# Projections of an adaLN layer: the first scale and shift applied after the transpose, by ScalarE, instead of before it, by VectorE

## The chip, the cores and the metric

One NeuronCore of a Trainium2 chip runs the whole kernel. The metric is the device time of one execution in microseconds (us), the median of several runs.

## The reference

Two adaLN layers on x of 2 batches of 2048 tokens, 256 features. Only the head of layer 0 matters here:

```python
mod = (silu(L0_c) @ L0_wmod).reshape(2, 6, 1, 256)   # L0_c is 2 x 256, L0_wmod 256 x 1536
sa, ca, ga, sb, cb, gb = mod[:, 0], ..., mod[:, 5]
h = layernorm(x) * (1 + ca) + sa                     # one scale and one shift a batch and feature
Q, K, V = h @ W_q.T, h @ W_k.T, h @ W_v.T            # then rotary embedding on Q and K
```

Causal attention with 16 heads of 16 features, a top-1 mixture of experts, and layer 1 (a Toeplitz mix and a top-2 mixture of experts) follow. All inputs are float32. Matrix products are made of rounded parts: a value is split into a part rounded to fp32r and the rest (`HI`, `LO`), and three of the four products are summed.

## The kernel before, in words

The program is a row of stages, each a block in which the five engines (TensorE: PE, VectorE: DVE, ScalarE: ACT, GpSimd: POOL, SyncE: SP, which issues most DMAs) run their own lists of instructions in order and meet by semaphores. The stages are `projections`, `attention`, `output_projection`, `top1_experts`, `layer1`, `routed_experts`, `combine`. The change lies in `projections` (L236 to L593) alone.

This stage works through 8 chunks of 512 tokens (4 a batch), each held as 4 tiles of 128 tokens by 256 features. For chunk i:

- DVE `statistics(i)` takes mean and variance (L372, then small ones at L142 to L148); POOL `deviation(i)` (L345) makes 1/sqrt.
- DVE `norm(i)` calls `normalize`: four `tensor_scalar` (L183) subtract the mean and divide, then `tensor_tensor` over 128x1024 multiplies by the scale (L187) and another adds the shift (L188). Scale and shift lie in `mods[0]`, the same row on all 128 partitions.
- PE `turn(i)` (L525) transposes the 8 blocks of h into the PSUM tile `p_t` (features on partitions, tokens along the row).
- ACT `round_hT(i)` (L457) copies `p_t` to `hT` HI, rounding; DVE `rest_of_hT(i)` (L391) subtracts HI from `p_t` to give LO.
- PE `product(i, qk)` (L537) makes q (qk 0) or k (qk 1) in 24 matmuls of 512 columns, 12 for each of the two summands `s` of the rotation; and V (L557), 24 of 256 columns.
- DVE `rotate` (L398) multiplies the PSUM result by cos or sin; POOL `add` (L334) sums the two into `rem`; then `rem` is split in three bf16 parts by ACT (L472), DVE `split` (L405), ACT (L476) and POOL `split_off` (L340). SP stores parts (L301) and V (L296) to HBM.

The order on DVE in `chunk(i)` is: norm(i+1), split(i-1, 1), rotate(i, 0) twice, rest_of_hT(i+1), statistics(i+2), rotate(i, 1) for s 0, split(i, 0), rotate(i, 1) for s 1. ACT does round_hT(i+1), take_v(i) (L465), then the splits; in chunks 4 to 6 it then issues the loads for the first stage of attention (`load_first_stage`), which need the stored parts of batch 0. PE does product(i, 0), V(i), turn(i+1), product(i, 1). In the first chunk all of these wait in addition for the start-up work.

Start-up: SP loads c, the first third of wmod (L311), x, the weights, the other two thirds of wmod, and the tables. DVE spreads silu(c) over 128 columns (`cb`, four `tensor_scalar` of 128x128 at L429), so that PE's products with wmod (L581, float32, 512 of its columns for each n of `halves`, in four passes) come out alike on all partitions; they are written to `pm`, which is the PSUM tile of V, and ACT copies them to `mods[0]` (L500). There are six such halves: (b, 0) gives sa and ca, (b, 1) ga and sb, (b, 2) cb and gb. Four are made before turn(0), two after it. PE's V product of chunk 0 waits until all are copied. `add_one` (L376) adds one to ca, later to cb.

At the end of the stage the first 12 maxima of attention (`early_maxima`) are already made, on data that the ACT-issued loads bring.

Of the kernel before, what the change touches and what calls it, by code (L numbers as in the profile page):

```python
# [25 lines left out]
P = 128  # L26
KT = D // P
CH = 512
# [150 lines left out]
def normalize(nc, k, own, i, h, scale, shift, done):  # L179


    for u in range(TPC):
        own.add(nc.vector.tensor_scalar(h[:, u, :], k.x[:, at(i * TPC + u, 1, 1), :].rearrange("p o d -> p (o d)"),  # L183
                                        k.mean[:, at(i * TPC + u, 1, 1)], k.rstd[:, at(i * TPC + u, 1, 1)],
                                        ALU.subtract, ALU.mult))
    own.wait()
    own.step(nc.vector.tensor_tensor(h, h, scale, ALU.mult))  # L187
    nc.vector.tensor_tensor(h, h, shift, ALU.add).then_inc(done, 1)  # L188
# [43 lines left out]
def projections(nc, a, k):  # L232

    with ExitStack() as stack:
# [18 lines left out]
        cT, silu_c = (small[:, 2 * P + n * KT * B:2 * P + (n + 1) * KT * B].rearrange("p (k b) -> p k b", k=KT) for n in range(2))  # L253
        pm = p_v[:, :, :].rearrange("p u d -> p (u d)").rearrange("p (n c) -> p n c", n=2)
        early = [p_t[:, :, :], p_qk[:, 0, :, :]]
        halves = [(0, 0), (1, 0), (0, 1), (0, 2), (1, 1), (1, 2)]
        c_loaded, wm_loaded = m.sem("c_loaded"), [m.sem(f"wm_loaded{n}") for n in range(2)]
        constants_loaded, x_in = m.sem("constants_loaded"), [m.sem(f"x_in{i}") for i in range(NCH)]
        c_ready, cb_ready, mod_ones_set = m.sem("silu_c_ready"), m.sem("cb_ready"), m.sem("mod_ones_set")
# [23 lines left out]
        def last_chunk(i):  # L283
            return i == NCH - 1

        with nc.Block() as block:
# [78 lines left out]
            def _(dve):  # L365
# [9 lines left out]
                def add_one(which):  # L375
                    c.step(nc.vector.tensor_scalar(k.mods[0][:, :, which, :], k.mods[0][:, :, which, :], 1.0, None, ALU.add))  # L376

                def norm(i):
                    dve.wait_ge(rstd_ready, i + 1)
                    if not first(i):  # L380
                        dve.wait_ge(turned, i)
                    normalize(nc, k, c, i, h[:, :, :], k.mod(0, i // CPS, CA), k.mod(0, i // CPS, SA), h_ready)

                def rest_of_w(n):
                    cols = columns[n]
# [2 lines left out]

                def rest_of_hT(i, par):
                    dve.wait_ge(hT_high, i + 1)  # L390
                    nc.vector.tensor_tensor(hT[:, par, LO, :, :], p_t[:, :, :], hT[:, par, HI, :, :],  # L391
                                            ALU.subtract).then_inc(hT_ready, 1)

                def rotate(i, qk, halves_of):
# [13 lines left out]
                def chunk(i, par):  # L408
                    if not last_chunk(i):
                        norm(i + 1)  # L410
                    if first(i):
                        dve.wait_ge(trig_loaded, 16)
                    else:
                        split(i - 1, 1)
                    rotate(i, 0, range(2))
                    if not last_chunk(i):
                        rest_of_hT(i + 1, 1 - par)
                    if i + 2 < NCH:
                        statistics(i + 2)
                    rotate(i, 1, range(1))  # L420
                    split(i, 0)
                    rotate(i, 1, range(1, 2))

                nc.vector.memset(ones, 1.0).then_inc(mod_ones_set, 1)
                dve.wait_ge(mod_ones_set, 1)
                dve.wait_ge(c_ready, 1)
                for kt in range(KT):
                    for b in range(B):
                        nc.vector.tensor_scalar(cb[:, kt, b, :], ones, silu_c[:, kt, b:b + 1], None, ALU.mult).then_inc(cb_ready, 1)  # L429
                statistics(0)  # L430
                dve.wait_ge(mod_copied, B)
                add_one(CA)
                norm(0)
                rest_of_w(0)
                statistics(1)
# [5 lines left out]
                dve.wait_ge(constants_loaded, 16 * 2)  # L441
                c.add(nc.vector.tensor_copy(k.identb[:, :], k.ident[:, :]))
                c.add(nc.vector.tensor_copy(k.masks[:, :], masks))
                dve.wait_ge(mod_copied, len(halves))
                add_one(CB)
                all_chunks(chunk)
                for u in range(EARLY):
                    if u == 2:
# [4 lines left out]
            @block.scalar  # L453
            def _(act):
                def round_hT(i, par):
                    act.wait_ge(turned, i + 1)
                    nc.scalar.activation(hT[:, par, HI, :, :], p_t[:, :, :], ACT.Copy).then_inc(hT_high, 1)  # L457

                def take_v(i):
                    act.wait_ge(v_psum, i + 1)  # L460
# [41 lines left out]

                act.wait_ge(c_loaded, 16)
                nc.scalar.activation(silu_c, cT, ACT.Silu).then_inc(c_ready, 1)
                for n in range(B):
                    take_mods(n)
                act.wait_ge(w_loaded, 16)
                for cols in columns:
                    nc.scalar.activation(w[:, HI, :, cols], raw[:, :, cols], ACT.Copy).then_inc(w_high, 1)
                for n in range(B, 2 * B):  # L510
                    take_mods(n)
                round_hT(0, 0)
                for n in range(2 * B, len(halves)):
                    take_mods(n)
                all_chunks(chunk)

# [1 line left out]
            def _(pe):  # L518
# [23 lines left out]
                def chunk(i, par):  # L542
                    pe.wait_ge(hT_ready, i + 1)
                    if first(i):
                        pe.wait_ge(w_ready, 1)
                    product(i, par, 0)
                    if first(i):
                        pe.wait_ge(mod_copied, len(halves))
                        pe.wait_ge(w_ready, 3)
                    elif last_chunk(i):  # L550
                        product(i, par, 1)
                    if not first(i):
                        pe.wait_ge(va_ready, i)
                    for u in range(TPC):
                        for kt in range(KT):
                            for wp, hp in PRODUCTS:
                                last = nc.tensor.matmul(p_v[:, u, :], hT[:, par, hp, kt, u * P:(u + 1) * P],  # L557
                                                        w[:, wp, kt, 4 * D:5 * D],
                                                        start=(kt, wp, hp) == (0, HI, HI),
                                                        stop=(kt, wp, hp) == (KT - 1, LO, HI))  # L560
                    last.then_inc(v_psum, 1)
                    if not last_chunk(i):
                        turn(i + 1)
                        product(i, par, 1)
# [9 lines left out]

                def modulate(n):
                    b, half = halves[n]
                    pe.wait_ge(wm_loaded[half > 0], 16)
                    if n >= 2:
                        pe.wait_ge(mod_copied, n - 1)
                    for kt in range(KT):  # L580
                        last = nc.tensor.matmul(pm[:, n % 2, :], cb[:, kt, b, :], wm[:, kt, 2 * half * D:(2 * half + 2) * D],  # L581
                                                start=kt == 0, stop=kt == KT - 1)
                    last.then_inc(mod_product, 1)

                pe.wait_ge(cb_ready, KT * B)
                for n in range(2 * B):
                    modulate(n)
                pe.wait_ge(constants_loaded, 16 * 2)
                turn(0)
                for n in range(2 * B, len(halves)):  # L590
                    modulate(n)
                all_chunks(chunk)
                early_maxima()  # L593

# [1982 lines left out]
```

## Time and profile before

| What | us |
|---|---|
| median of 3 runs (2446.16 to 2450.19) | 2449.44 |
| profiled execution, its time | 2455.55 |
| its span | 2453.8 |
| busy in the span: PE | 2206.0 |
| DVE | 1715.6 |
| ACT | 1273.1 |
| POOL | 878.1 |

The span runs from the first to the last instruction of the profiled execution; 1.75 us lie outside it. The projections take about the first 188 us of the span. Busy time of PE is modelled for pipelined matmuls, so a busy PE may still have slack. A line of the timeline has the start and the length of an instruction (or of a merged run of alike ones, then with a count), its engine and line, the tiles written and read with their shapes, and in brackets how long the engine stood idle before it and what ended that. "ACTq", "SPq" and "POOLq" are the sequencers that issue DMAs. "PEld" is the load of weights into TensorE.

### The profile page before, as it was taken

The numbers are of one execution on the slowest core, as the hardware profiler recorded it, in microseconds if no ns is written. First come the engines' busy times: TensorE is split into PE (matmuls) and PEld (weight loads), VectorE is DVE, ScalarE is ACT, GpSimd is POOL, SyncE is SP. The second block draws the span as 40 slices with busy tenths as digits, with TensorE's granted clock in tenths as the row PEclk, the third lists the DMA queues.
The fourth block names the chain that finished last, engine by engine and source line by source line (L and its number), as shares of the span: only waits on it lengthen the run. The fifth ranks groups of instructions, "written<-read, shape, count | busy, mean of one in ns | idle before, by whom it ended". The sixth has DMA issues, their size and how long they took to land. (4 is left out here: it accounts for less than half of the span.)

```text
span 2453.8 us, 38931 instructions
## 1 busy us (share of the span) xinstructions
PE 2206.0 (90%) x12968; PEld 1400.8 (57%) x12968; DVE 1715.6 (70%) x2748; ACT 1273.1 (52%) x2452; POOL 878.1 (36%) x1057
## 2 busy tenths in 40 slices
PE   7878999999999999988999599963999999999991
PEld 5752333333333333326777456643888888888881
DVE  8968787878788787815788778774555555555566
ACT  3332767777677767773333244421555555555552
POOL 3543321313131220212555512454345444445350
PEclk9986999999999999998999798875999999999996
DMA  6499116345261711003000100013534443444326
GB/s 212 142 205 127 26 62 112 89 105 96 81 122 54 148 71 45 1 16 118 1 0 0 34 0 5 35 41 121 189 135 140 143 136 136 171 157 142 134 74 219
DMA packets 140246, 235.78 MB, mean 96 GB/s; under 512 B 14816, under 2 KB 105568, under 8 KB 138656
## 3 DMA queue, kind: packets, MB, share of 16 engines
q1 hardware_dynamic: 124416, 181.18, 21.4%
q0 software_dynamic: 14544, 48.05, 11.1%
q10 hardware_dynamic: 1104, 4.20, 1.2%
q8 instruction: 105, 1.72, 0.3%
q14 instruction: 77, 0.63, 0.1%
HBM read 150.58 MB, written 82.42 MB: 95 GB/s over the span
## 5 line engine op out<-in xcount | busy, mean ns | idle before, releaser
L228 DVE TENSOR_REDUCE tile_max<-p_m 128x2 f32<-128x1024 f32 (+1 forms) x628 | 642.5, 1065 | 137.1 <-PE p_m L220 69.2
L929 ACT ACTIVATE probs<-p_s 128x512 f32<-128x512 f32 (+3 forms) x1280 | 596.4, 534 | 242.4 <-PE p_s L834 237.0
L2210 PE MATMUL p_up<-f_xT,f_w 128*128 128x512 f32 (+1 forms) x2304 | 464.8, 351 | 7.1 <-DVE f_w L2344 3.6
L2210 PEld LDWEIGHTS p_up<-f_xT,f_w 128*128 128x128 f32 x2304 | 368.9, 189 | 59.6 <-issue 9.2
L776 POOL TENSOR_SCALAR_AFFINE_SELECT probs<-probs 128x128 f32<-128x128 f32 x512 | 145.9, 294 | 700.9 <-ACT probs L929 692.4
L834 PE MATMUL p_s<-qa,ka 99*128 99x512 bf16 (+3 forms) x1280 | 352.0, 351 | 13.2 <-ACT probs L929 6.9
L217 PE MATMUL p_m<-ka,qa 96*128 96x512 bf16 (+1 forms) x1256 | 353.0, 364 | 11.2 <-DVE tile_max L228 5.0
L2379 POOL TENSOR_TENSOR f_w<-f_raw,f_w 128x1024 fp32r<-128x1024 f32 x95 | 230.9, 2440 | 365.2 <-ACT f_w L2265 365.2
L848 PE MATMUL p_o<-probs,va 128*32 128x512 f32 (+3 forms) x2560 | 301.5, 541 | 1.3 <-issue 1.0
L2225 PE MATMUL p_y<-f_w,f_hidden 128*128 128x256 f32 x1872 | 252.5, 281 | 15.1 <-DVE f_y L2339 14.2
L2225 PEld LDWEIGHTS p_y<-f_w,f_hidden 128*128 128x128 f32 x1872 | 237.8, 188 | 30.0 <-issue 21.7
L217 PEld LDWEIGHTS p_m<-ka,qa 96*128 96x128 bf16 x1256 | 108.2, 99 | 238.0 <-DVE tile_max L228 133.9
L2326 DVE SCALAR_TENSOR_TENSOR f_gate<-p_up,f_b,f_gate 128x512 f32<-128x512 f32 (+1 forms) x192 | 124.7, 649 | 166.3 <-ACT f_gate L2278 162.9
L834 PEld LDWEIGHTS p_s<-qa,ka 99*128 99x128 bf16 x1280 | 110.5, 98 | 223.6 <-ACT probs L929 143.0
L2330 DVE TENSOR_TENSOR f_hidden<-f_gate,f_hidden 128x512 fp32r<-128x512 f32 (+1 forms) x192 | 141.7, 738 | 118.7 <-ACT f_hidden L2283 112.0
L2278 ACT ACTIVATE f_gate<-p_up,f_b 128x512 f32<-128x512 f32 (+1 forms) x192 | 116.3, 606 | 154.9 <-PE p_up L2210 148.3
L1283 PE MATMUL p_e<-w_expert,c_hT 128*128 128x512 f32 x768 | 195.1, 404 | 0.0
L2283 ACT ACTIVATE f_hidden<-f_gate 128x512 fp32r<-128x512 f32 (+1 forms) x192 | 105.9, 552 | 160.3 <-DVE f_gate L2326 157.0
L1283 PEld LDWEIGHTS p_e<-w_expert,c_hT 128*128 128x128 f32 x768 | 140.6, 190 | 29.6
L2265 ACT ACTIVATE f_w<-f_raw 128x1024 fp32r<-128x1024 f32 x144 | 150.5, 1045 | 2.7 <-DMA f_raw<-in_W 2.2
L1709 PE MATMUL p_uv<-l_xnT,w_uv 128*128 128x512 f32 x256 | 112.7, 597 | 0.0
L537 PE MATMUL p_qk<-hT,wqkv 128*128 128x512 f32 x384 | 96.0, 409 | 14.8 <-DVE rot L398 14.7
(278 smaller groups left out, 2625.4 us busy)
## 6 DMA issues: line engine op xcount, KB each, us to landing
x_slots<-mods SPq DMA_DIRECT2D x73, 516.0 KB, 4.3
f_raw<-in_W SPq DMA_DIRECT2D x24, 1024.0 KB, 11.2
f_raw<-in_W1a SPq DMA_DIRECT2D x23, 1024.0 KB, 6.4
f_raw<-in_W1b SPq DMA_DIRECT2D x23, 1024.0 KB, 8.7
qk_scr<-parts SPq DMA_DIRECT2D x48, 256.0 KB, 2.8
qa<-qk_scr POOLq DMA_DIRECT2D x42, 256.0 KB, 15.7
ka<-qk_scr POOLq DMA_DIRECT2D x42, 256.0 KB, 17.6
v_scr<-wqkv_raw SPq DMA_DIRECT2D x32, 256.0 KB, 3.8
```

The lines of the kernel that those rows point to most:

```text
L217: last = nc.tensor.matmul(out[:, hh, 0:width], qa[0:QROWS, hd, q0:q0 + P], ka[0:QROWS, hd, bank * CH:bank * CH + width], start=True, stop= ...
L228: return nc.vector.tensor_reduce(out=k.tile_max[:, 2 * hp:2 * hp + 2, i, bank], in_=products[:, :, 0:width], op=ALU.max, axis=AX.X)
L776: last = nc.gpsimd.affine_select(block_, block_, pattern=[[1, P]], compare_op=ALU.is_ge, fill=0.0, base=0, channel_multiplier=-1)
L834: nc.tensor.matmul(p_s[:, s_bank(x, buf), lo:CH], ka[buf][0:QROWS + SPLIT, h, j * P:(j + 1) * P], qa[buf][0:QROWS + SPLIT, h, c * CH + lo: ...
L848: last = nc.tensor.matmul(p_o[VW * h:VW * (h + 1), lo:CH], va[buf][:, j, VW * h:VW * (h + 1)], probs[:, (buf * UNITS + n) % NPROBS, h, lo: ...
L929: nc.scalar.activation(probs[:, (buf * UNITS + n) % NPROBS, h, lo:CH], p_s[:, s_bank(("exp", HG * n + h), buf), lo:CH], ACT.Exp, scale=DH ...
L1283: last = nc.tensor.matmul(out, hT[:, par, hp, kt, :], weights(wp, kt), start=(kt, wp, hp) == (0, HI, HI), stop=(kt, wp, hp) == (KT - 1, LO ...
L2210: last = nc.tensor.matmul(p_up[:, f % 2, ab, 0:size], w1[:, wh, ab * KT + kt, f * P:(f + 1) * P], xT[:, t % 2, xh, kt, 0:size], start=(kt, ...
L2225: last = nc.tensor.matmul(p_y[:, u, :], hidden[:, (FB * t + f) % NHID, hh, u * P:(u + 1) * P], w2[:, wh, f, :], start=(f, wh, hh) == (0, H ...
L2265: nc.scalar.activation(piece_part(q, HI), piece_raw(q, par), ACT.Copy).then_inc(w_high, 1)
L2330: nc.vector.tensor_tensor(hidden[:, (n - 1) % NHID, LO, 0:size], gate[:, f % 2, 0:size], hidden[:, (n - 1) % NHID, HI, 0:size], ALU.subtra ...
L2379: nc.gpsimd.tensor_tensor(piece_part(q, LO), piece_raw(q, t % 2), piece_part(q, HI), ALU.subtract).then_inc(w1_ready, 1)
```

## The change

In layer 0's first norm, h now holds only the normalized x. The scale and the shift are needed with features on partitions: `modT` (128 x 2 x 2 x 2). PE makes them directly as eight float32 products with two result columns each (wmod block as weights, silu(c) as the moving side), DVE copies them from PSUM and adds one to the scale. ACT, which took the transposed chunk with one rounding copy, now applies them with two `Identity` instructions of 128x512 (one for each half of the features, scale and shift as columns of one value a partition) into a new SBUF tile `whole_hT`, waits for both, and rounds from `whole_hT`; DVE takes the rest from `whole_hT`, no longer from the PSUM tile. The two halves (b, 0) are no longer made the old way. The other four are moved on PE behind product(0, 0), the four L429 instructions on DVE behind the casts of the constants, and `add_one(CB)` into chunk 0 behind rotate(0, 0).

```diff
-        halves = [(0, 0), (1, 0), (0, 1), (0, 2), (1, 1), (1, 2)]
+        halves = [(0, 1), (0, 2), (1, 1), (1, 2)]
+        modT = m.sb("modT", [P, 2, KT, B])
+        whole_hT = m.sb("whole_hT", [P, KT, CH])
+        p_modT = p_v[:, 0, 0:2 * KT * B].rearrange("p (w k b) -> p w k b", w=2, k=KT)
...
@@ DVE, norm(i) @@
-                    normalize(nc, k, c, i, h[:, :, :], k.mod(0, i // CPS, CA), k.mod(0, i // CPS, SA), h_ready)
+                    for u in range(TPC):
+                        t = i * TPC + u
+                        last = nc.vector.tensor_scalar(h[:, u, :], k.x[:, t, :], k.mean[:, t:t + 1], k.rstd[:, t:t + 1],
+                                                       ALU.subtract, ALU.mult)
+                    last.then_inc(h_ready, 1)
...
@@ DVE, rest_of_hT(i, par) @@
-                    nc.vector.tensor_tensor(hT[:, par, LO, :, :], p_t[:, :, :], hT[:, par, HI, :, :],
+                    nc.vector.tensor_tensor(hT[:, par, LO, :, :], whole_hT[:, :, :], hT[:, par, HI, :, :],
                                             ALU.subtract).then_inc(hT_ready, 1)
...
@@ DVE, chunk(i, par) @@
                     rotate(i, 0, range(2))
+                    if first(i):
+                        dve.wait_ge(mod_copied, len(halves))
+                        add_one(CB)
                     if not last_chunk(i):
                         rest_of_hT(i + 1, 1 - par)
...
@@ DVE, start-up @@
                 nc.vector.memset(ones, 1.0).then_inc(mod_ones_set, 1)
-                dve.wait_ge(mod_ones_set, 1)
-                dve.wait_ge(c_ready, 1)
-                for kt in range(KT):
-                    for b in range(B):
-                        nc.vector.tensor_scalar(cb[:, kt, b, :], ones, silu_c[:, kt, b:b + 1], None, ALU.mult).then_inc(cb_ready, 1)
+                dve.wait_ge(modT_product, 1)
+                nc.vector.tensor_scalar(modT[:, CA, :, :], p_modT[:, CA, :, :], 1.0, None, ALU.add).then_inc(modT_ready, 1)
+                nc.vector.tensor_copy(modT[:, SA, :, :], p_modT[:, SA, :, :]).then_inc(modT_ready, 1)
                 statistics(0)
-                dve.wait_ge(mod_copied, B)
-                add_one(CA)
                 norm(0)
...
                 c.add(nc.vector.tensor_copy(k.masks[:, :], masks))
-                dve.wait_ge(mod_copied, len(halves))
-                add_one(CB)
+                dve.wait_ge(mod_ones_set, 1)
+                for kt in range(KT):
+                    for b in range(B):
+                        nc.vector.tensor_scalar(cb[:, kt, b, :], ones, silu_c[:, kt, b:b + 1], None, ALU.mult).then_inc(cb_ready, 1)
                 all_chunks(chunk)
...
@@ ACT, round_hT(i, par) @@
+                    b = i // CPS
                     act.wait_ge(turned, i + 1)
-                    nc.scalar.activation(hT[:, par, HI, :, :], p_t[:, :, :], ACT.Copy).then_inc(hT_high, 1)
+                    if first(i):
+                        act.wait_ge(modT_ready, 2)
+                    else:
+                        act.wait_ge(hT_ready, i)
+                    for kt in range(KT):
+                        nc.scalar.activation(whole_hT[:, kt, :], p_t[:, kt, :], ACT.Identity, scale=modT[:, CA, kt, b:b + 1],
+                                             bias=modT[:, SA, kt, b:b + 1]).then_inc(modulated, 1)
+                    act.wait_ge(modulated, KT * (i + 1))
+                    nc.scalar.activation(hT[:, par, HI, :, :], whole_hT[:, :, :], ACT.Copy).then_inc(hT_high, 1)
...
@@ ACT, start-up @@
-                for n in range(B):
-                    take_mods(n)
...
-                for n in range(B, 2 * B):
-                    take_mods(n)
                 round_hT(0, 0)
-                for n in range(2 * B, len(halves)):
+                for n in range(len(halves)):
                     take_mods(n)
...
@@ PE, chunk(i, par) @@
                     product(i, par, 0)
                     if first(i):
+                        pe.wait_ge(cb_ready, KT * B)
+                        pe.wait_ge(modT_ready, 2)
+                        for n in range(len(halves)):
+                            modulate(n)
                         pe.wait_ge(mod_copied, len(halves))
                         pe.wait_ge(w_ready, 3)
...
@@ PE, start-up @@
-                pe.wait_ge(cb_ready, KT * B)
-                for n in range(2 * B):
-                    modulate(n)
+                pe.wait_ge(c_ready, 1)
+                pe.wait_ge(wm_loaded[0], 16)
+                for which in (SA, CA):
+                    for mb in range(KT):
+                        col = which * D + mb * P
+                        for kt in range(KT):
+                            last = nc.tensor.matmul(p_modT[:, which, mb, :], wm[:, kt, col:col + P], silu_c[:, kt, :],
+                                                    start=kt == 0, stop=kt == KT - 1)
+                last.then_inc(modT_product, 1)
                 pe.wait_ge(constants_loaded, 16 * 2)
                 turn(0)
-                for n in range(2 * B, len(halves)):
-                    modulate(n)
                 all_chunks(chunk)
```

## Rows read from the trace of the kernel before

**Rows 1.** One stretch: length, busy PE, PEld, DVE, ACT, POOL, clock, DMA share, GB/s.
```profile
67.00:85.00 18.00, 15.04 (x79) 12.54 (x80) 17.86 (x24) 6.06 (x6) 10.23 (x5) 1.00 0.45 146
```

**Rows 2.** Timeline of one steady chunk, 60 to 79 us.
```profile
60.19 5.29 DVE L183 TENSOR_SCALAR h<-x,mean,rstd 128x256 f32<-128x256 f32 x4
60.31 2.29 POOL L340 TENSOR_TENSOR parts<-rem,parts 128x1024 bf16<-128x1024 f32 x1 [2.33 <-ACT parts L476]
62.56 2.44 POOL L334 TENSOR_TENSOR rem<-rot 128x1024 f32<-128x1024 f32 x1
...
65.51 1.22 DVE L187 TENSOR_TENSOR h<-h,mods 128x1024 f32<-128x1024 f32 x1
...
67.91 1.22 DVE L405 TENSOR_TENSOR rem<-rem,parts 128x1024 f32<-128x1024 f32 x1
...
69.17 1.06 ACT L476 ACTIVATE parts<-rem 128x1024 bf16<-128x1024 f32 x1 [3.07 <-DVE rem L405]
70.13 1.01 ACT L457 ACTIVATE hT<-p_t 128x1024 fp32r<-128x1024 f32 x1
...
71.31 1.22 DVE L391 TENSOR_TENSOR hT<-p_t,hT 128x1024 fp32r<-128x1024 f32 x1
72.42 2.39 POOL L334 TENSOR_TENSOR rem<-rot 128x1024 f32<-128x1024 f32 x1
...
73.88 0.95 DVE L142 TENSOR_TENSOR mean<-stats 128x4 f32<-128x4 f32 x1
...
78.83 5.29 DVE L183 TENSOR_SCALAR h<-x,mean,rstd 128x256 f32<-128x256 f32 x4
```

**Rows 3.** Timeline, the same small DVE instruction in a later chunk.
```profile
130.62 0.17 DVE L142 TENSOR_TENSOR mean<-stats 128x4 f32<-128x4 f32 x1
```

**Rows 4.** Timeline of DVE and POOL in the routed experts.
```profile
1782.63 1.41 DVE L2330 TENSOR_TENSOR f_hidden<-f_gate,f_hidden 128x256 fp32r<-128x256 f32 x1 [0.48 <-ACT f_hidden L2283]
...
1781.35 7.48 POOL L2379 TENSOR_TENSOR f_w<-f_raw,f_w 128x1024 fp32r<-128x1024 f32 x3 [5.95 <-ACT f_w L2265]
```

**Rows 5.** Groups of ACT by form: busy us, mean ns.
```profile
L1640 ACT ACTIVATE v_sb<-p_uv,b_uv 128x512 f32<-128x512 f32 x32 | 21.9, 684 | 46.4 <-PE p_uv L1709 46.4
...
L500 ACT ACTIVATE mods<-p_v 128x512 f32<-128x512 f32 x6 | 3.6, 596 | 13.5 <-PE p_v L581 13.5
```

**Rows 6.** Landing of the DMA of line 311, issued at 1.26 us.
```profile
DMA to landing us min/median/max: 3.7/3.7/3.7
```

**Rows 7.** Timeline of the start-up, 2 to 46 us.
```profile
2.80 5.63 DVE L429 TENSOR_SCALAR qa<-va 128x128 f32<-128x128 f32 x4 [1.73 <-ACT va L504]
...
10.79 1.04 POOL L345 TENSOR_TENSOR rstd<-ve,neghalf 128x4 f32<-128x4 f32 x1 [2.89 <-DVE ve L148]
...
20.65 3.60 PE L581 MATMUL p_v<-qa 128*128 128x512 f32 x8
...
24.13 5.74 PE L537 MATMUL p_qk<-hT,wqkv 128*128 128x512 f32 x24
...
29.70 3.03 PE L557 MATMUL p_v<-wqkv,hT 128*128 128x256 f32 x24
...
33.74 11.45 PE L537 MATMUL p_qk<-hT,wqkv 128*128 128x512 f32 x48
...
34.80 1.22 DVE L391 TENSOR_TENSOR hT<-p_t,hT 128x1024 fp32r<-128x1024 f32 x1
```

**Rows 8.** PE after idle times: one product, its stretch (TensorE's granted clock 0.66), and narrow float32 products.
```profile
161.56 8.22 PE L537 MATMUL p_qk<-hT,wqkv 128*128 128x512 f32 x24 [5.45 <-DVE rot L398]
...
160.00:170.00 10.00, 8.44 (x28) 6.85 (x29) 5.18 (x6) 2.64 (x3) 4.47 (x2) 0.66 1.05 151
...
1495.68 1.57 PEld L1734 LDWEIGHTS l_small<-l_wl,l_zT 128*128 128x128 f32 x7 [1.51 <-ACT l_zT L1631]
```

**Rows 9.** Timeline of chunk 6, POOL and ACT.
```profile
155.04 2.37 POOL L334 TENSOR_TENSOR rem<-rot 128x1024 f32<-128x1024 f32 x1
...
158.06 1.06 ACT L472 ACTIVATE parts<-rem 128x1024 bf16<-128x1024 f32 x1 [5.20 <-DMA qk_scr<-parts]
```

More of the change, by code:

```diff
@@ L255, in projections @@
         early = [p_t[:, :, :], p_qk[:, 0, :, :]]
-        halves = [(0, 0), (1, 0), (0, 1), (0, 2), (1, 1), (1, 2)]
+        halves = [(0, 1), (0, 2), (1, 1), (1, 2)]
+        modT = m.sb("modT", [P, 2, KT, B])
+        whole_hT = m.sb("whole_hT", [P, KT, CH])
+        p_modT = p_v[:, 0, 0:2 * KT * B].rearrange("p (w k b) -> p w k b", w=2, k=KT)
+        modT_product, modT_ready, modulated = m.sem("modT_product"), m.sem("modT_ready"), m.sem("a_modulated")
         c_loaded, wm_loaded = m.sem("c_loaded"), [m.sem(f"wm_loaded{n}") for n in range(2)]
@@ L576, in modulate @@
                     b, half = halves[n]
-                    pe.wait_ge(wm_loaded[half > 0], 16)
+                    pe.wait_ge(wm_loaded[1], 16)
                     if n >= 2:
```

## The prediction

> **What bounds the kernel now.** I first read the busy time by engine in stretches. The chain that ended last reaches back only through the last stage, so it can't tell what a change in the first stage is worth. The stages meet at barriers, and what the projections lose or gain moves everything behind them by as much. In 18 us of steady chunks DVE is busy for 17.86, PE for 15.04, POOL for 10.23 and ACT for 6.06 [rows 1]. So DVE sets the pace, it seems, and the change takes work from DVE. But busy is not the same as working, so the next view is the timeline of one chunk, which repeats every 78.83 - 60.19 = 18.64 us [rows 2].
>
> There the four normalizing instructions of norm take 5.29 us. Alone they would take about 0.33 us each: the first one's share, before POOL starts at 60.31. The others end when POOL's two operations do (L334 ends at 62.56 + 2.44 = 65.00, the norm at 65.48). DVE and POOL take turns: who starts first holds something the other needs. It isn't only this form. L142, which adds two columns that both lie in SBUF, takes 0.95 us when it meets L334 [rows 2] and 0.17 when POOL is idle [rows 3]. L391, which reads PSUM and SBUF, takes its normal 1.22 us though POOL's L334 starts under it at 72.42 [rows 2]. And in the experts L2330, a rest of rounding with both inputs in SBUF, starts at 1782.63 under a POOL operation and takes 1.41 us [rows 4].
>
> **The change, part by part. First, the steady chunk.** I follow chunk 2 from the norm at 60.19.
>
> *Removed from DVE:* L187 and its twin L188, 1.22 us each [rows 2]. They end just ahead of L405 (split of the chunk before) at 67.91. Without them L405 can't move to 65.48. It needs ACT's L472 (as long as L476, 1.06), which needs L334's end at 65.00. So L405 starts at 66.12, a gain of 1.79 and not 2.5; ACT's L476 starts at 67.38 instead of 69.17. Late next is thus the way through POOL and ACT.
>
> *Added on ACT:* the rounding copy L457 starts 0.96 after L476 (69.17 to 70.13) [rows 2], so ACT reaches the new work at 68.34. A 128x512 activation from PSUM takes 0.60 with no column operand and 0.68 with a bias column [rows 5]. The new ones have two columns, scale and bias; no row shows that form. Bounds are 0.60 and, with 0.09 for each column, 0.78. I take 0.78, since one column already shows 0.09. Two of them, the second starting 0.1 before the first ends, then the wait for both and the copy of 1.02: 68.34 + 0.68 + 0.78 + 0.03 + 1.02 + 0.03 = 70.88. With no cost for columns it is 70.5. The Trainium skill (ScalarE: Activation LUTs, section What ACT_TABLE_LOAD costs) says that each pointer operand adds about 93 ns; the one-column row agrees.
>
> *Changed on DVE:* the rest of hT now reads two SBUF tiles. POOL's L334 starts 3.25 us after L476 (72.42 - 69.17) [rows 2], at 70.63 now, 0.25 ahead of DVE's 70.88, and it holds until 73.02. The rest then ends about 1.1 later, at 74.1; before, it ended at 72.53. So 1.79 earlier has become 1.6 later. L142 no longer meets L334, which gives back 0.95 - 0.17 = 0.78. What follows on DVE, statistics, rotate and split, keeps its lengths. **One chunk: + 1.6 - 0.8 = + 0.8 us.** PE and its turn(i+1) keep ahead: h is ready at 65.48, and ACT comes to it only at 68.34. Chunks 1 to 5 pay this: 5 x 0.8 = + 4.0. Chunk 6 has no statistics, and ACT is late there by its own DMA issues: the norm's 1.8 is gained, and for the blocked rest I give back 1.0 (bounds 0 and 1.6): - 0.8. At its end ACT waited for a store until 158.06, although POOL was through at 157.41 [rows 9], so 0.6 of the shift is absorbed: - 0.6. The loads issued by ACT and the stores behind it move along with it, since ACT issues them in order.
>
> **Second, the start-up.** Early on the new order wins. The first wmod block lands at 1.26 + 3.7 = 4.96 [rows 6]. Eight float32 products are 16 passes; 7 weight loads of such a product take 1.57 [rows 8], 0.22 each, so 3.6: 8.6. Two small DVE copies, 0.35: 8.9. Statistics and the root took from 8.43 to 11.83 [rows 7], 3.4: 12.3. Norm 1.4: 13.7. Eight transposes, 1.1 to 2.0, since PE has stood idle; 2.0: 15.7. ACT 2.6: 18.3. Rest 1.2: product(0, 0) starts at 19.5 instead of 24.13 [rows 7]. The L429s, 5.63 us for four before since POOL was filling memory [rows 7], are now at about 24 and hidden by PE's product; without that cover they would cost at most as much. The deleted add and copies were on this way and are in it. The new small waits are hidden: cb, modT and hT are long ready.
>
> Then it loses. PE did the float32 products of wmod while it waited for others; now four of them stand between product(0, 0) and V, and V writes their tile. PE: product(0, 0), 8.2 as in the row after an idle time, where the granted clock was 0.66 on average, between the two levels 1.2 and 2.4 GHz [rows 8]; 5.7 if the clock is up [rows 7]. I take 8.2, since PE here also stands idle ahead of it: 27.7. Four halves are 16 passes; 8 take 3.60 [rows 7], so 7.2: 34.9. ACT's last copy 0.6 [rows 5]: 35.5. V and turn(1) took from 29.70 to 33.74 [rows 7], 4.0: 39.5. ACT 2.6: 42.1. There the rest of hT(1) starts, which started at 34.80 [rows 7]. All that DVE does behind it waits: + 7.3. DVE is idle for over ten microseconds in front of it, also in its add_one, queued ahead of the rest. With both prices of the clock the term is 4.8 to 7.3.
>
> **Sum.** 7.3 + 4.0 - 0.8 - 0.6 = + 9.9 us. The profiled execution would go from 2455.55 to 2465.5. It is 6.1 above the median of the runs; on that median it is 2449.4 + 9.9 = 2459.3.
>
> **Rivals.**
> *DVE gets in first.* If the columns cost nothing on ACT, DVE asks at 70.5, before L334 starts at 70.63, and POOL waits instead. The rest then ends at about 71.8, L142 is blocked until L334's late end (about 74.1), and a chunk comes to - 0.7. In chunks 1 to 4 that is 4 x 1.5 less (chunk 5 has ACT's DMA issues ahead of the rounding, so there DVE comes late all the same): + 3.9, 2453.3. The 0.68 against 0.60 speaks against it [rows 5]; it decides by 0.1 to 0.25 us.
> *Not slower: the two reads don't collide.* If this form of subtraction ran beside POOL as L391 does, the rest would end at 72.1 and L142 would be free: - 1.3 a chunk. From 7.3 that takes 5 x 1.3 and some 1.2 in chunk 6: - 0.4, 2449.0, and with the clock up - 2.9. The point from which it decides is 0.6 us of wait in the rest. L2330 and L142 speak against it [rows 2 to 4]; that the change does free 2.4 us of DVE a chunk speaks for it. The Trainium skill (SBUF — State Buffer, section Who interferes with whom) says that two SBUF inputs contend with a GpSimd instruction that reads SBUF; by that rule this rival falls, and the rows agree.
> *Start-up cheaper.* With the clock up, 7.4 instead of 9.9: 2456.8; it is in the forecast's own range, 2455 to 2462.
>
> **How the numbers follow.** The forecast has 0.66, DVE first 0.12, no collision 0.09; 0.13 is left for what I don't see, in the last chunks' DMA traffic above all, on both sides. A measurement of this kernel can tell 0.2%, 4.9 us, from no change: same is 2444.5 to 2454.3. Same gets most of the two rivals and a little of the rest, 0.24; slower 0.69; faster 0.07. The range of 8 in 10 reaches from 2451 (it takes in DVE first) to 2463.5 (a chunk dearer by 0.5, and disturbed loads).
>
> **What would show it.** Right: L391 in the changed kernel at 3.3 to 3.4 us when it follows ACT's copy in chunks 1 to 4, ending 1.1 behind POOL's L334; a period of 19.4 us; the first of these rests at 42; product(0, 0) at 19.5. Wrong: a rest of 1.2 us and a period under 18 (a rival holds); L581's passes done before 30; the gain of L405 below 1.8; or the first stage's end moved by much less than the chunks are.

## The result, and the profile after

The changed kernel takes 2454.06 us (median of 11 runs, 2452.67 to 2461.0) beside 2450.19 for the kernel before (median of 11 on the same chip). The ratio of the runs is 1.0022, 95% interval 1.0013 to 1.0031: 3.2 to 7.6 us slower, 5.4 in the middle (the two medians alone are 3.9 apart). One run of the kernel before, at 8573.94 us, was a slow one and isn't in the ratio, which compares fast runs. A difference of 0.2% is small, but the interval leaves no change out. The profiled execution took 2454.83 us, of which the span is 2453.1. The forecast was 2459.3, in a range from 2451.0 to 2463.5.

The page's first part, for the kernel after. DVE is busy for 19.5 us less than before (1715.6), ACT for 10.8 us more, and the kernel is still slower:

```profile
PE 2199.6 (90%) x12976; PEld 1401.8 (57%) x12976; DVE 1696.1 (69%) x2733; ACT 1283.9 (52%) x2466; POOL 876.3 (36%) x1057
```

In the kernel after, the line numbers have moved: norm is L388, the rest of hT L399, rotate L406, DVE's split L413, POOL's add L338 and split_off L344, ACT's two new instructions L472, the rounding copy L475, ACT's splits L490 and L494, product L551, V L575, turn L539, the halves L599.

**A steady chunk.** Timeline of the kernel after from 49 to 69 us, which answers to [rows 2]:

```profile
49.37 5.29 DVE L388 TENSOR_SCALAR h<-x,mean,rstd 128x256 f32<-128x256 f32 x4
...
55.31 1.23 DVE L413 TENSOR_TENSOR rem<-rem,parts 128x1024 f32<-128x1024 f32 x1 [0.65 <-ACT parts L490]
...
56.57 1.06 ACT L494 ACTIVATE parts<-rem 128x1024 bf16<-128x1024 f32 x1 [1.29 <-DVE rem L413]
57.53 1.43 ACT L472 ACTIVATE whole_hT<-p_t,modT 128x512 f32<-128x512 f32 x2
...
58.99 1.06 ACT L475 ACTIVATE hT<-whole_hT 128x1024 fp32r<-128x1024 f32 x1
59.80 2.41 POOL L338 TENSOR_TENSOR rem<-rot 128x1024 f32<-128x1024 f32 x1
60.09 3.21 DVE L399 TENSOR_TENSOR hT<-whole_hT,hT 128x1024 fp32r<-128x1024 f32 x1 [1.29 <-ACT hT L475]
...
64.65 0.17 DVE L142 TENSOR_TENSOR mean<-stats 128x4 f32<-128x4 f32 x1
...
68.81 5.28 DVE L388 TENSOR_SCALAR h<-x,mean,rstd 128x256 f32<-128x256 f32 x4
```

The two instructions L187 and L188 are gone, but the norms are 68.81 - 49.37 = 19.44 us apart where they were 18.64. The rest L399 takes 3.21 us instead of 1.22. It starts 0.29 after POOL's L338 and ends 63.30 - 62.21 = 1.09 after it: it has done next to nothing while POOL ran. L142, which met L334 before and took 0.95, now takes 0.17.

The same in sums. Groups of DVE and ACT by form over the projections, first after, then before (busy us, mean ns of one, then idle time):

```profile
L399 DVE TENSOR_TENSOR hT<-whole_hT,hT 128x1024 fp32r<-128x1024 f32 x8 | 17.9, 2240 | 19.2 <-ACT hT L475 19.2
L142 DVE TENSOR_TENSOR mean<-stats 128x4 f32<-128x4 f32 x8 | 1.3, 165 | 0.3
...
L472 ACT ACTIVATE whole_hT<-p_t,modT 128x512 f32<-128x512 f32 x16 | 11.6, 772 | 10.3 <-PE p_t L539 10.3
```
```profile
L391 DVE TENSOR_TENSOR hT<-p_t,hT 128x1024 fp32r<-128x1024 f32 x8 | 9.7, 1218 | 1.3 <-ACT hT L457 1.3
L142 DVE TENSOR_TENSOR mean<-stats 128x4 f32<-128x4 f32 x8 | 4.5, 558 | 0.3
```

**The start-up.** Timeline of the kernel after, 12 to 44 us, which answers to [rows 7]:

```profile
12.41 1.38 DVE L388 TENSOR_SCALAR h<-x,mean,rstd 128x256 f32<-128x256 f32 x4 [1.23 <-POOL rstd L349]
...
18.48 1.22 DVE L399 TENSOR_TENSOR hT<-whole_hT,hT 128x1024 fp32r<-128x1024 f32 x1 [1.36 <-ACT hT L475]
19.76 8.62 PE L551 MATMUL p_qk<-hT,wqkv 128*128 128x512 f32 x24 [3.88 <-DVE hT L399]
...
28.23 7.03 PE L599 MATMUL p_v<-qa 128*128 128x512 f32 x16
...
35.94 3.14 PE L575 MATMUL p_v<-wqkv,hT 128*128 128x256 f32 x24 [0.69 <-ACT mods L518]
...
42.63 1.23 DVE L399 TENSOR_TENSOR hT<-whole_hT,hT 128x1024 fp32r<-128x1024 f32 x1 [6.28 <-ACT hT L475]
```

Product(0, 0) starts at 19.76 instead of 24.13, yet the first rest of chunk 1 starts at 42.63 instead of 34.80: a lead of 4.4 us has turned into a delay of 7.8. What lies between is one long product (8.62) and the 16 passes of the four halves (7.03).

**The end of the stage.** The first maximum products of attention, which wait for the barrier behind the projections and which all of attention follows. "The stage's end" is their start. Timeline of before and of after:

```profile
188.61 1.86 PE L217 MATMUL p_m<-ka,qa 96*128 96x512 bf16 x4 [0.79 <-PEq L286]
```
```profile
199.25 1.87 PE L217 MATMUL p_m<-ka,qa 96*128 96x512 bf16 x4 [0.79 <-PEq L290]
```

So the first stage is longer by 10.6 us, and the whole kernel by 5.4. The experiments are about both halves of that: what makes the 10.6, and where the other 5 go.

### The profile page after: what moved, and what is told of

Read it like the earlier page. It is cut to its first block and busy times, and to the rows that moved or that the text cites. A ratio compares the mean times of both kernels' runs of the same rounds, so it can differ in the third digit from the quotient of the medians.

```text
span 2453.1 us, 38955 instructions
## 1 busy us (share of the span) xinstructions
PE 2199.6 (90%) x12976; PEld 1401.8 (57%) x12976; DVE 1696.1 (69%) x2733; ACT 1283.9 (52%) x2466; POOL 876.3 (36%) x1057
## 5 line engine op out<-in xcount | busy, mean ns | idle before, releaser
L551 PE MATMUL p_qk<-hT,wqkv 128*128 128x512 f32 x384 | 102.5, 428 | 28.2 <-DVE rot L406 24.3
```

## The experiments

The first stage's end is given against 188.7, the mean of four profiles of the kernel before (188.6, 189.1, 189.0, 188.1). The end comes from one profiled execution of each kernel, unlike the ratios; three of the kernel after gave 199.2, 197.8 and 199.1.

### The product of ACT kept in PSUM

Does DVE wait because it reads two SBUF tiles? ACT writes the scaled and shifted chunk back over `p_t`; the rounding copy and the rest read it there. Everything else stays.

```diff
-    nc.scalar.activation(whole_hT[:, kt, :], p_t[:, kt, :], ACT.Identity, ...)
+    nc.scalar.activation(p_t[:, kt, :], p_t[:, kt, :], ACT.Identity, ...)
...
-    nc.scalar.activation(hT[:, par, HI, :, :], whole_hT[:, :, :], ACT.Copy)
+    nc.scalar.activation(hT[:, par, HI, :, :], p_t[:, :, :], ACT.Copy)
...
-    nc.vector.tensor_tensor(hT[:, par, LO, :, :], whole_hT[:, :, :], hT[:, par, HI, :, :],
+    nc.vector.tensor_tensor(hT[:, par, LO, :, :], p_t[:, :, :], hT[:, par, HI, :, :],
```

> The changed kernel, but ACT writes the scaled and shifted chunk back into its PSUM tile, and the rounding copy and DVE's rest read it there. Theory (two SBUF inputs of DVE's rest wait for POOL's L338): the rest falls from 3.2 or 2.3 us to 1.2 in chunks 1 to 5, the period of a steady chunk from 19.4 to 17.2 to 17.6 us, and the first stage ends 9 to 12 us earlier than in the changed kernel; whole kernel 2442 to 2447 us. Rival 1 (the way through POOL and ACT sets the period): the rest is 1.2 us but the period stays above 19 and nothing is gained. Rival 2 (the stores and loads of chunks 5 to 7 bound the end): period as in the theory, but the stage ends less than 6 us earlier.

Measured: 2448.29 us, ratio to before 0.9986 (0.9975 to 0.9997). The stage ends at 189.0, 10.2 us earlier than in the kernel after: inside the expected 9 to 12. The whole kernel was expected at 2442 to 2447 and missed that by 1.3 us. Timeline of DVE, steady chunks:

```profile
60.13 1.22 DVE L399 TENSOR_TENSOR hT<-p_t,hT 128x1024 fp32r<-128x1024 f32 x1 [1.23 <-ACT hT L475]
...
66.87 5.29 DVE L388 TENSOR_SCALAR h<-x,mean,rstd 128x256 f32<-128x256 f32 x4
...
77.53 1.22 DVE L399 TENSOR_TENSOR hT<-p_t,hT 128x1024 fp32r<-128x1024 f32 x1 [1.23 <-ACT hT L475]
...
84.27 5.29 DVE L388 TENSOR_SCALAR h<-x,mean,rstd 128x256 f32<-128x256 f32 x4
```

The rest is back at 1.22 us in every chunk, and the chunk takes 84.27 - 66.87 = 17.40 us, 2.04 less than after and 1.24 less than before. It starts as late behind ACT as in the kernel after (60.13 there 60.09), under the same POOL instruction, so it is where the chunk lies, in PSUM or in SBUF, that decides, not when the rest is asked for. With this, the move of scale and shift to ACT is worth 1.24 us in a steady chunk; the start-up's 7.9 us (first rest of chunk 1 at 42.73) eat it up.

### ACT without the two columns

Where both operands stay in SBUF, who waits? The two `Identity` instructions become plain copies: scale and shift are left out of layer 0's first norm.

```diff
-    nc.scalar.activation(whole_hT[:, kt, :], p_t[:, kt, :], ACT.Identity, scale=modT[...], bias=modT[...])
+    nc.scalar.activation(whole_hT[:, kt, :], p_t[:, kt, :], ACT.Copy)
```

> The changed kernel, but ACT's two instructions a chunk are plain copies: scale and shift are left out. A plain 128x512 copy takes 0.60 us, with two columns 0.77 was measured, so DVE's rest is asked for 0.35 us earlier, 0.06 ahead of the start of POOL's L338 instead of 0.29 behind it. Theory (who starts first of the two holds the other): where PE is at the full clock the rest takes 1.2 to 1.5 us instead of 3.2, L338 takes 3.2 to 3.6 instead of 2.4, L142 is blocked again (0.9 to 1.0), and the period is 17.8 to 18.1 us. Rival (the rest waits for POOL whoever starts first): the rest stays above 3 us and the period at 19.4.

Measured in one execution: 2446.97 us, the stage's end at 191.0. Timeline, steady chunks:

```profile
57.94 1.22 DVE L399 TENSOR_TENSOR hT<-whole_hT,hT 128x1024 fp32r<-128x1024 f32 x1 [0.93 <-ACT hT L474]
58.03 3.39 POOL L338 TENSOR_TENSOR rem<-rot 128x1024 f32<-128x1024 f32 x1
...
60.51 0.93 DVE L142 TENSOR_TENSOR mean<-stats 128x4 f32<-128x4 f32 x1
...
65.44 5.29 DVE L388 TENSOR_SCALAR h<-x,mean,rstd 128x256 f32<-128x256 f32 x4
...
83.31 5.29 DVE L388 TENSOR_SCALAR h<-x,mean,rstd 128x256 f32<-128x256 f32 x4
```

The same rest, with both operands in SBUF, takes 1.22 us when it starts 0.09 ahead of POOL, and now POOL's L338 takes 3.39 instead of 2.41. So neither engine has the right of way: the first to start holds. The period of 83.31 - 65.44 = 17.87 is what the first rival gave (18.64 - 0.7 = 17.94). So all four parts of the theory (rest, L338, L142, period) came out. What kept that rival from coming true is the price of the columns: 772 ns an instruction after, 590 in this run (group of L472 by form, `... x16 | 8.6, 590 | ...`), so 0.36 us for the two, against the 0.29 by which DVE came late after.

### The four halves ahead of the first product

Is the start-up's delay the place of the four halves? `cb` is made first on DVE again, PE makes the halves right behind turn(0), and `add_one(CB)` goes back ahead of the chunks.

```diff
@@ PE @@
                 turn(0)
+                pe.wait_ge(cb_ready, KT * B)
+                pe.wait_ge(modT_ready, 2)
+                for n in range(len(halves)):
+                    modulate(n)
                 all_chunks(chunk)
...
@@ PE, chunk(i, par), first(i) @@
-                        pe.wait_ge(cb_ready, KT * B)
-                        pe.wait_ge(modT_ready, 2)
-                        for n in range(len(halves)):
-                            modulate(n)
```

> The changed kernel, but the four old-style halves of wmod are made right behind turn(0) again, ahead of product(0, 0), with their spread columns made first on DVE. Theory (the four halves between product(0, 0) and V cost the start-up 7 us): V of chunk 0 starts at about 29 instead of 35.9, the first rest of chunk 1's hT at 35 to 36 instead of 42.6, all chunks behind it 6 to 7 us earlier with the period unchanged at 19.4; whole kernel 2446 to 2449 us. Rival (DVE's queue or the late clock holds the start-up): less than 3 us earlier.

Measured: 2449.51 us, ratio 1.0003 (0.9993 to 1.0013), the stage's end at 191.8, 7.4 us earlier than in the kernel after (6 to 7 was expected, and 2446 to 2449 us for the kernel: both slightly missed). Timeline of the start-up:

```profile
22.77 6.03 PE L551 MATMUL p_qk<-hT,wqkv 128*128 128x512 f32 x24
...
35.15 1.23 DVE L399 TENSOR_TENSOR hT<-whole_hT,hT 128x1024 fp32r<-128x1024 f32 x1 [5.10 <-ACT hT L475]
...
41.90 5.27 DVE L388 TENSOR_SCALAR h<-x,mean,rstd 128x256 f32<-128x256 f32 x4
...
61.31 5.29 DVE L388 TENSOR_SCALAR h<-x,mean,rstd 128x256 f32<-128x256 f32 x4
```

Product(0, 0) starts 3.0 us later than in the kernel after (22.77 against 19.76) and the rest of chunk 1 starts 7.5 earlier (35.15), 0.35 behind before. The halves now fill PE's wait for ACT and DVE (they start at 15.69, right behind turn(0)), and the product behind them takes 6.03 us and not 8.62. The chunks keep their 19.41.

### Both edits

> The two edits before together. Theory (the two losses are independent and add): the first stage ends 16 to 19 us earlier than in the changed kernel, whole kernel 2435 to 2441 us, and so faster than both kernels. Rival (the DMAs of chunks 5 to 7 bound the end of the stage): the chunks up to 5 gain 17 us, the end of the stage 12 or less; 2441 to 2446 us.

Measured: 2439.25 us (2437.78 to 2441.51), ratio 0.9957 (0.9943 to 0.9971), the stage's end at 181.5. Timeline:

```profile
35.09 1.22 DVE L399 TENSOR_TENSOR hT<-p_t,hT 128x1024 fp32r<-128x1024 f32 x1 [5.04 <-ACT hT L475]
...
52.49 1.23 DVE L399 TENSOR_TENSOR hT<-p_t,hT 128x1024 fp32r<-128x1024 f32 x1 [1.23 <-ACT hT L475]
...
69.88 1.23 DVE L399 TENSOR_TENSOR hT<-p_t,hT 128x1024 fp32r<-128x1024 f32 x1 [1.23 <-ACT hT L475]
```

The first rest of chunk 1 starts within 0.3 us of the kernel before (35.09 against 34.80), and a chunk takes 69.88 - 52.49 = 17.39. The two gains add, 10.2 + 7.4 = 17.6 in the stage against 17.7 measured (199.2 - 181.5). This version is faster than both kernels, than the one before by 7.1 to 14.0 us, and leaves nothing of the work out.

### A delay put into the kernel before

In the kernel after, some 5 us of the first stage's delay don't arrive at the end. Does a delay always lose something on the way? The kernel before, with DVE filling `va` seven times instead of once before chunk 0:

```diff
-                nc.vector.memset(va[:, :, :, :], 1.0).then_inc(ones_set, 1)
+                for n in range(7):
+                    dve.wait_ge(ones_set, n)
+                    nc.vector.memset(va[:, :, :, :], 1.0).then_inc(ones_set, 1)
...
-                        act.wait_ge(ones_set, 1)
+                        act.wait_ge(ones_set, 7)
```

> The kernel before with six more memsets of the same tile on DVE ahead of chunk 0, nothing else: 6 x 1.8 = 10.8 us of pure delay in the first stage. Theory (a delay in the first stage moves everything behind it by as much, stages meet at barriers): stage end and whole kernel + 10 to 11 us, about 2460. Rival (later stages give part of a delay back, as the two traces suggest, where a lag of 10.6 us at the start of attention is 5.2 at its end): + 4 to + 7 us, about 2455.

Timeline of DVE (`va` goes by the name of `wqkv_raw` here):

```profile
26.24 1.76 DVE L442 MEMSET wqkv_raw<- 128x2048 f32 x1 [0.49 <-DVE wqkv L387]
28.50 1.76 DVE L442 MEMSET wqkv_raw<- 128x2048 f32 x1 [0.49 <-DVE wqkv_raw L442]
...
49.15 1.22 DVE L391 TENSOR_TENSOR hT<-p_t,hT 128x1024 fp32r<-128x1024 f32 x1 [0.85 <-ACT hT L459]
```

Each further fill costs 28.50 - 26.24 = 2.26 us and not 1.8, since DVE stands idle for 0.49 ahead of each. So the delay put in is larger than meant: 49.15 - 34.80 = 14.4 us at the first rest of chunk 1, 14.6 at the stage's end (203.3). The kernel takes 2460.99 us, ratio 1.0043 (1.0027 to 1.0058): + 10.5 us, between 6.6 and 14.2. The + 10.5 fits the expected "about 2460" only by chance, since the expectation had a delay of 10 to 11 in mind. Measured against the 14.6, the middle is 4 us short here too, but the interval nearly reaches it.

### A small delay

The same edit with fills of four columns, `va[:, 0, 0, 0:4]`, for the first six.

> The kernel before with the same number of added DVE instructions and waits as the run with the long memsets, but of 4 columns each: 6 x 0.3 to 0.6 = 2 to 3.5 us in the first stage. Theory A (a delay in the first stage comes through in full): whole kernel + 2 to + 3.5 us, ratio 1.001. Theory B (what every variant shares, a shifted instruction stream on DVE, makes the later stages 3 to 5 us shorter): ratio 0.999 to 1.000 in spite of the delay.

Timeline of DVE:

```profile
25.21 0.71 DVE L442 MEMSET wqkv_raw<- 128x4 f32 x6
26.41 1.76 DVE L442 MEMSET wqkv_raw<- 128x2048 f32 x1 [0.49 <-DVE wqkv_raw L442]
```

2448.64 us, ratio 0.9994 (0.9982 to 1.0006). The six together take 0.71 us, though each waits for the one before it; the 0.49 ahead of the long fill is there in the kernel before too. The first rest of chunk 1 starts at 34.90, 0.1 later than before, and the stage ends at 188.6. The ratio lies in the range of theory B, but the delay of 2 to 3.5 us that was wanted didn't come about, and without it theory A would give 1.0000, which is inside the interval as well. So this run doesn't tell the two apart.

### The two kernels again

Before and after were run and timed once more, unchanged, to see how far executions of one kernel differ.

> The kernel before, unchanged, timed against itself. Open: outside the first stage every variant so far was 3 to 5 us shorter than before, even one whose first stage ended at the same time and one with nothing but memsets added. If this comparison has no bias: ratio 1.000 within 0.001. Rival (something in how the kernel before comes out in these comparisons, not the variants' code): 0.998 to 0.999.

> The changed kernel, unchanged, timed again beside before. If the first measurement held: ratio 1.0015 to 1.003, 4 to 7 us slower. Rival (the first stage's 10 us come through in full, the first measurement was low): 1.0035 to 1.0045.

Before against itself: ratio 1.0000 (0.9986 to 1.0013). After against before: 2456.9 us, 1.0024 (1.0014 to 1.0034), + 5.9 us; the first measurement gave + 5.4. Both ratios are as expected. Three more profiles, of one execution each:

> The kernel before, unchanged, profiled a second time. Open: the changed kernel's first stage ends 10.6 us later than before's in the trace, the whole kernel only 4 to 5. Theory (the first profile of before was an execution whose attention and later stages were long by chance): the first stage ends at 188 to 189 us again, attention is 3 to 6 us shorter than the first time, the time 2447 to 2452. Rival (the first stage itself varies and was short that time): the first stage ends 3 us or more later than 188.6.

> The kernel before, unchanged, a third profile, to see how far stages of one kernel vary between executions: the same expectations as for the second.

> The changed kernel, unchanged, profiled a second time. Theory: the first stage ends within 1 us of 199.2 again, since its chunks are set by instructions and not by chance; the later stages sum to within 3 us of the first time. Rival: the first stage's end moves by more than 3 us.

They took 2452.04, 2452.38 and 2458.83 us, with the stage's end at 189.1, 189.0 and 197.8. Attention, from its start to the start of the output projection, took 908.4 and 909.9 us in the two of before and 911.6 in the one of after, the longest of all thirteen profiles, while the first profile of after had 905.8, the shortest. The expectations were missed: attention in before was to be 3 to 6 us shorter than the first time (911.1) and was 2.7 and 1.2 shorter; the stage's end of after was to stay within 1 us and moved by 1.4, and what lies behind it was to stay within 3 us and is 5.4 longer. So stages of one kernel vary by some us with the execution, and a single pair of profiles doesn't show where the 5 us went.

## Why the prediction was right, and where its size was off

The sign, the mechanism in the first stage and the range were right; the point, + 9.9 us, is the first stage's figure and not the kernel's, where little more than half of it arrived. That the range still holds the result is in part luck, as told below.

**The steady chunk: right, step by step.** Counted from the start of norm, the prediction had L405's place at 5.93, ACT's second split at 7.19, ACT's new work at 8.15, POOL's add at 10.44, the rest asked for at 10.69 and ended at 13.9. After, these are 55.31 - 49.37 = 5.94, 7.20, 8.16, 10.43, 10.72 and 13.93. The chunk came out 19.44 - 18.64 = 0.80 us longer, as forecast. Two things carried it. The price of the two columns was set at its bound of 0.78 (772 ns measured; 0.60 would have let DVE in first, as the run without the columns shows). And a rest with two SBUF operands was taken to wait for POOL: the run with the chunk in PSUM confirms that as the cause, since only the place of the chunk was changed. One sign that the prediction named doesn't fit its own sum: it wanted a rest of 3.3 to 3.4 us, while 70.88 to 74.1 is 3.2, and 3.21 was measured. The Trainium skill's rule (SBUF — State Buffer, section Who interferes with whom) holds here: two SBUF inputs wait for POOL, 3.21 us, one in PSUM doesn't, 1.22.

**What the prediction didn't see in the chunk.** In three of the steady chunks of the kernel after, the rest starts later, for instance here (timeline):

```profile
66.77 7.30 PE L551 MATMUL p_qk<-hT,wqkv 128*128 128x512 f32 x24 [3.31 <-DVE rot L406]
...
79.23 2.41 POOL L338 TENSOR_TENSOR rem<-rot 128x1024 f32<-128x1024 f32 x1
...
80.43 2.30 DVE L399 TENSOR_TENSOR hT<-whole_hT,hT 128x1024 fp32r<-128x1024 f32 x1 [2.20 <-ACT hT L475]
```

PE waits for 3.31 us for DVE, its next product then takes 7.30 us instead of 5.7 (granted clock 0.77 over it, in the windows below, so part of it at the lower of the two levels, 1.2 GHz), and turn and ACT come late with it. The rest is asked for 0.9 us later and is shorter by as much (2.30), since it ends 1.09 behind POOL all the same. The wait behind POOL hides it; the period is unchanged.

**The start-up: right, 0.5 us short.** Forecast + 7.3, measured 42.63 - 34.80 = 7.8. Norm 12.41 (12.3), product(0, 0) at 19.76 (19.5) and 8.62 long (8.2), halves 7.03 (7.2), V at 35.94 (35.5), rest at 42.63 (42.1). The run with the halves ahead shows that the order of the start-up is nearly the whole of it: 7.5 of the 7.8 are gone. (It moves `cb` and `add_one(CB)` on DVE along with the halves on PE, so it doesn't part these.) The 8.2 was taken from a product at a granted clock of 0.66. The view of the clock seems to deny that here: it reads 1.00 over product(0, 0). Windows of the kernel after over product(0, 0) in two parts and over the slow product of a steady chunk (length, busy PE, clock, DMA share, GB/s):

```profile
19.76:26.00 6.24, 6.24 (x15) 1.00 1.09 385
26.00:28.38 2.38, 2.38 (x12) 1.00 0.41 143
...
66.77:74.07 7.30, 7.30 (x26) 0.77 0.28 94
```

The same in the run with the halves ahead, and over the product of [rows 8] in the kernel before, in two parts:

```profile
22.77:26.00 3.23, 3.23 (x15) 1.00 1.09 385
```
```profile
161.56:167.00 5.44, 5.44 (x13) 0.51 1.08 142
167.00:169.78 2.78, 2.78 (x15) 1.00 1.09 113
```

The DMA share is not what slows the product: at the same 1.09, 15 matmuls take 6.24 us in the one run and 3.23 in the other. And the clock fits after all. In product(0, 0) the matmuls behind the first follow each other every 0.43 us up to 25.9 and every 0.23 from then on, the same two steps as in the product of [rows 8], where they go with a granted clock of 0.5 and 1.00. The trace's record of the clock has its first entry, at full clock, at 25.98 us. Ahead of it there is none, and the view counts what is missing as 1.00. In the run with the halves ahead the first entry is at 16.91, and product(0, 0) has the step of 0.23 all through but for its first matmul. All this says that the 8.62 is a product that began at the lower level (1.2 GHz), as forecast; the 1.00 of the view says nothing about the time before the first entry.

**Chunk 6 and the stores: right in the sum alone.** Forecast - 1.4; measured 10.5 - 7.8 - 4.0 = - 1.3 with the stage's end at 199.2 against 188.7. Its two terms are not what happened. The last rest, in chunk 6, was to end 7.3 + 4.0 - 0.8 = 10.5 us later than before; in the first profiles it ended at 160.47 against 147.84, 12.6 later. Timeline of before and of after:

```profile
146.62 1.22 DVE L391 TENSOR_TENSOR hT<-p_t,hT 128x1024 fp32r<-128x1024 f32 x1 [0.62 <-ACT hT L457]
```
```profile
158.20 2.27 DVE L399 TENSOR_TENSOR hT<-whole_hT,hT 128x1024 fp32r<-128x1024 f32 x1 [2.22 <-ACT hT L475]
```

The 2.0 us between that and the stage's 10.6 were given back behind it. Why is open, and the - 1.3 is luck in part.

**The step that was off: "what the projections lose or gain moves everything behind them by as much".** The stage is 10 us longer (+ 9.9 forecast, + 10.5, + 9.1 and + 10.4 in three profiles), the kernel only 5.4 and 5.9. All timed kernels side by side, in us against the kernel before:

| kernel | stage's end | whole kernel (95%) | whole less stage |
|---|---|---|---|
| both edits | - 7.2 | - 10.5 (- 14.0 to - 7.1) | - 3.3 |
| product in PSUM | + 0.3 | - 3.4 (- 6.1 to - 0.7) | - 3.7 |
| halves ahead | + 3.1 | + 0.7 (- 1.7 to + 3.2) | - 2.4 |
| after | + 10.5 | + 5.4 (+ 3.2 to + 7.6) | - 5.1 |
| after, again | + 10.4 | + 5.9 (+ 3.4 to + 8.3) | - 4.5 |
| before with long fills | + 14.6 | + 10.5 (+ 6.6 to + 14.2) | - 4.1 |
| before with short fills | - 0.1 | - 1.5 (- 4.4 to + 1.5) | - 1.4 |
| before, again | - 0.6 | 0.0 (- 3.4 to + 3.2) | + 0.6 |

Read down, the step holds after all in one sense. From the first row to the long fills the stage moves by 21.8 us and the kernel by 21.0 (each end of that with an interval of some 3.5 us to both sides), so a shift is passed on about whole. What is left over is 2.4 to 5.1 us by which the kernels of the first six rows are shorter behind the first stage, whether it is longer or shorter than before; with these intervals it may be one constant. It is no absorbed delay: "both edits" has no delay to absorb.

The profiles show the same. From the stage's end to the end of the span it is 2261.1 to 2265.2 us in the four profiles of before, and 2253.1 to 2259.3 in the nine others. Two of these nine are the kernel before with fills added and nothing else (2256.7 and 2258.1), so the moved scale and shift isn't needed for it. Each figure is one execution. Attention has only a part of it: 908.4 to 911.1 us in the four, 907.8 in the mean of the nine (905.8 to 911.6). Windows of the two first profiles, before and after, over attention and over layer 1 but for its first 5.6 us (length, busy PE, PEld, DVE, ACT, POOL, clock, DMA share, GB/s):

```profile
188.60:1099.70 911.10, 880.83 (x5844) 313.70 (x5844) 698.19 (x861) 625.88 (x1345) 206.51 (x606) 0.97 0.36 76
...
1394.30:1705.60 311.30, 231.02 (x845) 155.68 (x845) 224.02 (x499) 111.49 (x274) 121.91 (x97) 0.81 0.09 32
```
```profile
199.20:1105.00 905.80, 877.94 (x5844) 313.52 (x5844) 698.02 (x861) 625.87 (x1346) 205.45 (x606) 0.97 0.35 77
...
1399.50:1706.50 307.00, 226.61 (x845) 152.37 (x845) 223.87 (x499) 111.43 (x274) 121.80 (x96) 0.82 0.09 32
```

The same instructions, with DVE, ACT and POOL busy within 1.1 us of before; PE is busy for 2.9 and 4.4 us less, at a granted clock that differs by 0.01 at most. But the second profile of after has 911.6 us in attention, so this pair shows a case and not the cause. **What stays open** is why all kernels that differ from before in the first stage are shorter behind it. It would have had to be known for the point; the range took it in only because its lower end had been drawn for another rival, which is luck.

The rivals: "DVE first" did not occur, and its mechanism and its 0.7 us a chunk were confirmed by the run without the columns (17.87 us a chunk). "No collision" is refuted by the 3.21 us. "Start-up cheaper" is refuted by the 8.62 us. The measured 2454.06 lies near the figure of "DVE first" (2453.3) for another reason altogether: who had only the two times would have taken the wrong one for right.

## What to carry to other kernels

Before work is moved off a busy engine, see whether the operands of what stays behind change their place: a `tensor_tensor` of DVE that read PSUM and now reads two SBUF tiles waits for POOL's, and 2.4 us of DVE's work saved became 0.8 us lost; writing the intermediate result back into PSUM gave 2.0 us a chunk back. What is moved on PE belongs where PE waits, not behind the first long product: a lead of 4.4 us at the first product was no lead at all for the engine that sets the pace. And check a forecast of a stage at the stage's end as well as at the kernel's, with the kernel before run against itself: the two differed here by 5 us.

## What the runs showed of the hardware that was not expected

- A lead of 0.09 us is enough in the taking of turns by DVE and POOL. Started 0.09 ahead, DVE's rest takes 1.22 and POOL's add 3.39; started 0.29 behind, 3.21 and 2.41.
- An ACT instruction of 128x512 can write over the PSUM tile that it reads, and is a little shorter for it: 742 ns as against 772 into SBUF, both with two columns (groups of L472 by form).
- DVE stands idle for 0.49 us ahead of each long fill (128x2048); six of them cost 2.9 us in the run with long fills. It isn't the wait for DVE's own last instruction that costs this: the fills of four columns wait in the same way and start 0.13 us apart.
- Work that fills an idle PE ahead of a product can pay for itself in part: with the halves ahead of it product(0, 0) took 6.03 us. With PE idle for 3.88 us ahead of it, it took 8.62, and its matmuls up to 25.9 us went at the step of the lower level.
- The view of the granted clock reads 1.00 where the record has no entry yet: up to 25.98 us in the kernel after, while the matmuls' step of 0.43 us shows the lower level.
